# Attention prologue as one stream by blocks, and the global query's row moved up

## The reference

```python
q = proj(Wq, bq) / np.float32(np.sqrt(dh)); k = proj(Wk, bk); v = proj(Wv, bv)
sb = jnp.einsum('bhnqd,bhnkd->bhnqk', qb, kb) + bias[:, None]      # band of three blocks of 128
sg = jnp.einsum('bhsd,bhgd->bhsg', q, kg)                          # the global key
probs = jax.nn.softmax(jnp.concatenate([sg, sb_flat], axis=-1), axis=-1)
out = einsum(probs band, vb) + einsum(probs global, vg)
sfull = jnp.einsum('bhgd,bhsd->bhgs', qg, k)                       # the global query's row over all keys
out = out.at[:, :, g].set(einsum(softmax(sfull), v))
return out @ Wo.T + bo
```

## Time and profile before

| | |
|---|---|
| runs | 1120.85, 1123.35, 1115.32 us; median 1120.85 |
| profiled execution | 1120.8 us; its span 1119.1 us |
| busy over the span | PE 885.0 us (79%), DVE 632.5 (57%), ACT 576.6 (52%), POOL 479.3 (43%) |
| mean granted TensorE clock | 0.888 of 2.4 GHz |
| first pass | first projection 30.3 us, first transposition 52.6, first transposed softmax unit (L1282) 80.6, output projection (L1322) 173.5 |
| first projections of the other passes | 232.6, 546.5, 750.5 us |

### The profile page before, as it was taken

The page is one execution under the profiler, slowest core; times in us unless marked ns, Lnnn a source line. Parts: engine busy times, 40 slices in busy tenths (PEclk is TensorE's granted clock), DMA queues, the critical chain, the costliest instruction groups (busy, mean ns, idle before and its releaser), DMA issues.

```text
span 1119.1 us, 24365 instructions
## 1 busy us (share of the span) xinstructions
PE 885.0 (79%) x8585; PEld 663.0 (59%) x8585; DVE 632.5 (57%) x2094; ACT 576.6 (52%) x1633; POOL 479.3 (43%) x676
## 2 busy tenths in 40 slices
PE   2789999977999896681688998968899998585376
PEld 0567766746776565551366766647677575374376
DVE  2688834457884525534478855328986353645343
ACT  1449983245798443121266985326599633312254
POOL 4008874310687634212205875520388554312233
PEclk9889999979999996685799999988999889577699
DMA  3200000020000004003210000002000000400221
GB/s 93 73 5 4 3 18 1 1 71 8 4 3 14 6 0 170 0 1 104 62 52 3 3 3 17 0 12 67 3 4 3 17 1 1 170 1 18 92 77 39
DMA packets 25974, 34.29 MB, mean 31 GB/s; under 512 B 7460, under 2 KB 19590, under 8 KB 25560
## 3 DMA queue, kind: packets, MB, share of 16 engines
q1 hardware_dynamic: 22234, 27.44, 7.9%
q0 software_dynamic: 2272, 4.74, 1.4%
q10 hardware_dynamic: 1338, 0.44, 0.2%
HBM read 26.64 MB, written 5.73 MB: 29 GB/s over the span
## 4 chain that ended last, share of the span: by engine, by line
PE 52%; DVE 19%; issue 14%; ACT 5%; DMA 4%; POOL 3%; SPq 2%; POOLq 1%; ACTq 1%; DVEq 0%
PE bank L1328 6%; PE bank L1180 5%; PE bank L1282 5%; PE bank L1338 4%; PE bank L1339 4%; PE bank L1238 4%; PE bank L1308 3%; DVE nmx L912 3%; PE bank L1285 2%; ACT p L709 2%; PE bank L1197 2%; PE bank L1241 2%; DMA xt<-xs 2%; PE bank L1213 2%; DVE nat L846 1%
## 5 line engine op out<-in xcount | busy, mean ns | idle before, releaser
L567 POOL TENSOR_TENSOR p<-p 128x384 f16<-128x384 f32 (+1 forms) x320 | 270.5, 859 | 101.1 <-ACT p L709 94.5
L912 DVE TENSOR_REDUCE nmx<-bank 128x1 f32<-128x384 f32 (+1 forms) x384 | 187.0, 511 | 39.3 <-PE bank L1241 34.9
L708 ACT ACTIVATE p<-bank 128x384 f32<-128x384 f32 (+1 forms) x384 | 174.3, 454 | 46.0 <-PE bank L1285 35.8
L709 ACT ACTIVATE p<-bank 128x384 f16<-128x384 f32 (+1 forms) x384 | 174.9, 455 | 0.0
L1282 PE MATMUL bank<-stack 103*128 103x128 bf16 x1056 | 145.8, 222 | 8.2 <-ACT p L709 4.6
L1285 PE MATMUL bank<-bandb,idb 128*128 128x128 bf16 x672 | 135.6, 222 | 0.0
L1238 PE MATMUL bank<-stack 100*128 100x384 bf16 (+1 forms) x384 | 120.9, 321 | 5.9 <-DVE nmx L912 4.5
L524 POOL TENSOR_TENSOR rstd<-ve,colc 128x1 f32<-128x1 f32 x96 | 54.2, 565 | 152.6 <-DVE ve L799 152.4
L1308 PE MATMUL bank<-vst,p 128*128 128x49 bf16 x2112 | 115.8, 185 | 0.1
L1282 PEld LDWEIGHTS bank<-stack 103*128 103x128 bf16 x1056 | 88.7, 99 | 31.4 <-issue 16.1
L1241 PE MATMUL bank<-bandb,idb 128*128 128x128 bf16 x672 | 102.3, 223 | 0.0
(11 more groups left out here) (252 smaller groups left out, 1890.4 us busy)
## 6 DMA issues: line engine op xcount, KB each, us to landing
mwbs<-in_mwb SPq DMA_DIRECT2D x2, 2064.0 KB, 8.7
mw2s<-in_mw SPq DMA_DIRECT2D x2, 2048.0 KB, 13.0
xt<-xs SPq DMA_DIRECT2D x23, 129.0 KB
w2s<-in_w SPq DMA_DIRECT2D x4, 576.0 KB
xs<-zrow SPq DMA_DIRECT2D x16, 129.0 KB
lnrow<-in_lnr SPq DMA_DIRECT2D x4, 480.0 KB
stack<-mtr SPq DMA_DIRECT2D x96, 3.0 KB
wqb<-in_wqkv SPq DMA_DIRECT2D x6, 218.2 KB
```

The costliest lines, as they stand in the source:

```text
L567: nc.gpsimd.tensor_tensor(p2[:, u % RING, 0:w], p32[:, u % RING, 0:w], p1[:, u % RING, 0:w], ALU.subtract).then_inc(p2_pool, 1)
L708: nc.scalar.activation(p32[:, s % RING, 0:w], ps[2 + s % 3][:, 0:w], ACT.Exp).then_inc(p32_ready, 1)
L709: nc.scalar.activation(p1[:, s % RING, 0:w], ps[2 + s % 3][:, 0:w], ACT.Exp).then_inc(p1_ready, 1)
L912: nc.vector.tensor_reduce(nmx[:, vn % 3, h:h + 1], nat_bank(v)[:, 0:w], AX.X, ALU.max, negate=True).then_inc(max_done, 1)
```

## The change

The stages ahead of unit 0 become one list by blocks. For j = 0 to 8 each engine does the part of block j's projection, then in four parts (`PARTS`) what belongs to the transposition of block j - 1, and from j = 3 on one of the 24 early steps behind each part (`early_step`). The `sg.meet()` behind the transpositions is gone; TensorE waits for single semaphores. v has one bank, `ps[2]`, the transpositions two, `ps[3]` and `ps[4]`, now eight heads of one block at a time; the early maxima two, `ps[6]` and `ps[7]`. Of the three groups of a block ScalarE evicts the first and third, VectorE the second. The rest after the first piece stays in PSUM, in place, and ScalarE reads the middle piece from there. The places of the pieces are reordered so that the repeated ones lie side by side; GpSimd makes the copies (`again`), in four instructions per block. `nat` holds two blocks and lies in the tile `hid` of the MLP. The global query's row keeps its start at step 72; its later steps move up (exponential to 85, norm 86, transposition and `f12` 88 and 89, product with v 90 to 93, mask product 95, column sums 97, copies 98). The two halves lie side by side in `f12`, so that one matmul does both, and the mask product takes two instructions over 24 rows, with `own` for `bm`. In the diff, cut to its core, 16 columns of indentation are left out.

```diff
-Q_ROWS = ((0, 16, 32), (48, 64), (80,))
-K_ROWS = ((0, 48, 80), (16, 64), (32,))
+HI, MID = 0, DH
+Q_HI, Q_MID, Q_LO = 2 * DH, 4 * DH, 5 * DH
+K_HI, K_MID, K_LO = 4 * DH, 2 * DH, 3 * DH
+HG = 8
+PARTS = 4
...
-            return ps[v % 4] if v < LEAD else ps[v % 2]
+            return ps[6 + v % 2] if v < LEAD else ps[v % 2]
+
+        def early_step(j, part):
+
+            return -LEAD + PARTS * (j - 3) + part if j >= 3 else None
...
-    sg.meet()
-    for s in range(-LEAD, U + 18):
+
+    def step(s):
...
+    for j in range(NB + 1):
+        if j < NB:
+            q, k = nat[:, j % 2, 0:H, :], nat[:, j % 2, H:2 * H, :]
+
+            def again(t, at, src):
+                return nc.gpsimd.tensor_copy(
+                    t[:, :, at:at + 2 * DH].rearrange("p h (i d) -> p h i d", d=DH),
+                    t[:, :, src:src + DH].unsqueeze(2).to_broadcast([P, H, 2, DH]))
+
+            pool.wait_ge(qk_hi, j + 1)
+            again(q, Q_HI, HI)
+            again(k, K_HI, HI)
+            pool.wait_ge(qk_mid, j + 1)
+            nc.gpsimd.tensor_copy(q[:, :, Q_MID:Q_MID + DH], q[:, :, MID:MID + DH])
+            nc.gpsimd.tensor_copy(k[:, :, K_MID:K_MID + DH], k[:, :, MID:MID + DH]).then_inc(qk_again, 1)
+        for part in range(PARTS):
+            if early_step(j, part) is not None:
+                step(early_step(j, part))
+    for s in range(0, U + 18):
+        step(s)
...
-    for n in range(NB):
-        act.wait_ge(qk_mm, n + 1)
-        nc.scalar.activation(nat[:, n, :, 0:DH],
-                             ps[n % 2][:, 0:2 * D].rearrange("p (h d) -> p h d", d=DH),
...
-    for k in range(0, 2 * H, 2):
-        act.wait_ge(tr_mm, k + 1)
-        nc.scalar.activation(stack[0:NPIECE, k, :], psb[4 + k % 4][0:NPIECE, :],
-                             ACT.Copy).then_inc(ev_act, 1)
-    sg.meet()
-
-    for s in range(-LEAD, U + 18):
-        if s == ROW + 14:
+
+    def step(s):
+        if s == ROW + 13:
...
-        if s == ROW + 19:
+        if s == ROW + 16:
             act.wait_ge(ft_mm, 1)
-            nc.scalar.activation(f1[:, :, :], ps[0][:, 0:NB * H].rearrange("p (n h) -> p n h", h=H),
+            nc.scalar.activation(f12[:, :, 0, :], ps[0][:, 0:NB * H].rearrange("p (n h) -> p n h", h=H),
...
-        if s == U + 7:
+        if s == U + 2:
...
+    def evacuate(b, g):
+        act.wait_ge(tr_mm, 3 * b + g + 1)
+        nc.scalar.activation(
+            stack[0:NPIECE, g * HG:(g + 1) * HG, blk(b)],
+            psb[3 + (3 * b + g) % 2][0:NPIECE, :].rearrange("p (h t) -> p h t", t=P),
+            ACT.Copy).then_inc(ev_act, 1)
+
+    for j in range(NB + 1):
+        if j < NB:
+            act.wait_ge(qk_mm, j + 1)
+            if j >= 2:
+                act.wait_ge(tr_mm, 3 * (j - 1))
+            nc.scalar.activation(nat[:, j % 2, :, HI:HI + DH],
+                                 ps[j % 2][:, 0:2 * D].rearrange("p (h d) -> p h d", d=DH),
+                                 ACT.Copy).then_inc(qk_hi, 1)
+            act.wait_ge(v_mm, j + 1)
+            nc.scalar.activation(vst[:, j, :, 0:DH], ps[2][:, 0:D].rearrange("p (h d) -> p h d", d=DH),
+                                 ACT.Copy).then_inc(v_hi, 1)
+        for part in range(PARTS):
+            if part == 1 and j < NB:
+                act.wait_ge(qk_rest, j + 1)
+                nc.scalar.activation(nat[:, j % 2, :, MID:MID + DH],
+                                     ps[j % 2][:, 0:2 * D].rearrange("p (h d) -> p h d", d=DH),
+                                     ACT.Copy).then_inc(qk_mid, 1)
+                act.wait_ge(v_rest, j + 1)
+                nc.scalar.activation(vst[:, j, :, DH:2 * DH],
+                                     ps[2][:, 0:D].rearrange("p (h d) -> p h d", d=DH),
+                                     ACT.Copy).then_inc(v_mid, 1)
+            if part in (1, 3) and j >= 1:
+                evacuate(j - 1, part - 1)
+            if early_step(j, part) is not None:
+                step(early_step(j, part))
+    for s in range(0, U + 18):
+        step(s)
...
+    def global_key():
+        dve.wait_ge(kb_out, 16 * H)
+        dve.wait_ge(rows_in, 32)
+        dve.wait_ge(ev_act, 2)
+        dve.wait_ge(ev_dve, 1)
...
+                                ALU.mult, ALU.add).then_inc(glob_ready, 1)
+
+    def global_value():
+        dve.wait_ge(v0_mm, 1)
+        for g in range(2):
+            ins = nc.vector.tensor_tensor(v0d[:, g, :], ps[6 + g][0:2 * H, 0:GW], own[:, g, :], ALU.mult)
+        ins.then_inc(v0_ready, 1)
+
...
-        if s == ROW + 16:
+        if s == ROW + 14:
             dve.wait_ge(f_exp, 2)
...
-        if s == ROW + 20:
+        if s == ROW + 17:
             dve.wait_ge(f1_ready, 1)
-            nc.vector.tensor_tensor(f2[:, :, :], ps[0][:, 0:NB * H].rearrange("p (n h) -> p n h", h=H),
-                                    f1[:, :, :], ALU.subtract).then_inc(f2_ready, 1)
-        if s == U + 4:
+            nc.vector.tensor_tensor(f12[:, :, 1, :], ps[0][:, 0:NB * H].rearrange("p (n h) -> p n h", h=H),
+                                    f12[:, :, 0, :], ALU.subtract).then_inc(f2_ready, 1)
+        if s == U - 1:
             dve.wait_ge(og_mm, 1)
+
+            def by_piece(t):
+                return t.rearrange("p (h w) -> p h w", w=VW)[:, :, 0:3 * DH].rearrange(
+                    "p h (i d) -> p i h d", d=DH)
+
             for g in range(2):
-                v_ = ps[1 - g][0:H, 0:HH * VW].rearrange("p (h w) -> p h w", w=VW)
-                for i in range(3):
-                    ins = nc.vector.tensor_tensor(
-                        heads(og[:, i, :])[:, half(g), :], v_[:, :, i * DH:(i + 1) * DH],
-                        heads(bm[0:H, :])[:, half(g), :], ALU.mult)
+                ins = nc.vector.tensor_tensor(
+                    og[:, :, g * HH * DH:(g + 1) * HH * DH].rearrange("p i (h d) -> p i h d", d=DH),
+                    by_piece(ps[1 - g][0:2 * H, 0:GW]), by_piece(own[:, g, :]), ALU.mult)
             ins.then_inc(og_ready, 1)
...
+    for j in range(NB + 1):
+        if j == 3:
+            global_key()
+        if j < NB:
+            q, k = nat[:, j % 2, 0:H, :], nat[:, j % 2, H:2 * H, :]
+            r, rv = heads(ps[j % 2][:, 0:2 * D]), heads(ps[2][:, 0:D])
+            dve.wait_ge(qk_hi, j + 1)
+            nc.vector.tensor_tensor(r, r, nat[:, j % 2, :, HI:HI + DH], ALU.subtract).then_inc(qk_rest, 1)
+            dve.wait_ge(v_hi, j + 1)
+            nc.vector.tensor_tensor(rv, rv, vst[:, j, :, 0:DH], ALU.subtract).then_inc(v_rest, 1)
+        if j == 2:
+            global_value()
+        for part in range(PARTS):
+            if part == 1 and j < NB:
+                dve.wait_ge(qk_mid, j + 1)
+                nc.vector.tensor_tensor(q[:, :, Q_LO:Q_LO + DH], r[:, 0:H, :], q[:, :, MID:MID + DH], ALU.subtract)
+                nc.vector.tensor_tensor(k[:, :, K_LO:K_LO + DH], r[:, H:2 * H, :], k[:, :, MID:MID + DH],
+                                        ALU.subtract).then_inc(qk_lo, 1)
+                dve.wait_ge(v_mid, j + 1)
+                nc.vector.tensor_tensor(vst[:, j, :, 2 * DH:3 * DH], rv, vst[:, j, :, DH:2 * DH],
+                                        ALU.subtract).then_inc(v_lo, 1)
+            if part == 2 and j >= 1:
+                dve.wait_ge(tr_mm, 3 * (j - 1) + 2)
+                nc.vector.tensor_copy(
+                    stack[0:NPIECE, HG:2 * HG, blk(j - 1)],
+                    psb[3 + (3 * (j - 1) + 1) % 2][0:NPIECE, :].rearrange("p (h t) -> p h t", t=P)).then_inc(ev_dve, 1)
+            if early_step(j, part) is not None:
+                step(early_step(j, part))
+    for s in range(0, U + 18):
+        step(s)
...
+    def project(j):
+        if j >= 2:
+            pe.wait_ge(qk_lo, j - 1)
+        mm(ps[j % 2][:, 0:2 * D], xa[:, blk(j)], wqa[:, 0:2 * D], start=True, stop=False)
...
+        if j >= 1:
+            pe.wait_ge(v_lo, j)
+        mm(ps[2][:, 0:D], xa[:, blk(j)], wqa[:, 2 * D:3 * D], start=True, stop=False)
+        mm(ps[2][:, 0:D], xb[0:DHI + 1, blk(j)], wqb[0:DHI + 1, 2 * D:3 * D], start=False,
            stop=True).then_inc(v_mm, 1)
...
+    def turn(b, g):
+        if g == 0:
+            pe.wait_ge(qk_lo, b + 1)
+            pe.wait_ge(qk_again, b + 1)
+            if b >= 1:
+                pe.wait_ge(ev_dve, b)
+        else:
+            if 2 * b + g - 1 > 0:
+                pe.wait_ge(ev_act, 2 * b + g - 1)
+        for h in range(HG):
+            ins = nc.tensor.transpose(psb[3 + (3 * b + g) % 2][0:NPIECE, blk(h)], nat[:, b % 2, g * HG + h, :],
+                                      idb[:, :])
         ins.then_inc(tr_mm, 1)
-    sg.meet()
...
-        if s == ROW + 18:
+        if s == ROW + 16:
...
-            if s != ROW + 22 + n // 2:
+            if s != ROW + 18 + n // 2:
                 continue
             if n == 0:
                 pe.wait_ge(f2_ready, 1)
             for g in range(2):
-                for ft in (f1, f2):
```

(45 more changed lines are left out.)

106 lines of the change are left out of this document (20 added, 86 removed).

## The result

| | before | after |
|---|---|---|
| median of 16 runs each | 1122.3 us | 1110.5 us |
| ratio | | 0.988, 95% interval 0.986 to 0.990 |
| profiled execution, its span | 1120.8, 1119.1 us | 1108.6, 1106.8 us |

The change makes the kernel 1.2% faster. The forecast was 1090 us, 31 us less than before; 12 came. The range held the time; the gain was less than half of the forecast.

What follows compares the result with a forecast made beforehand. Three engines took turns as the bound before the first softmax unit, then the global row's serial chain at the end. Stream 23.3 us plus tail 8 us made 31.3 off 1120.8: forecast 1090 us, range 1072 to 1118.

Steps and rivals of the forecast that it cites:

- The pace of the stream: Projections, transpositions and maxima as one stream: the order of work, not any engine's sum, sets 5.0 us per block.
- Rivals 1 and 3: Stream: 1, chain in block longer, period 5.8 us, 1113 us, chance 0.15; 3, TensorE-bound, period 4.5 us, 1074 us, 0.15.
- rival 4: Before the first softmax unit: the DMA of the maxima's rows, 3 us later, replaces the engines as bound; 1101 us.
- Its length: First projection to first softmax unit: 44.2 us for 50.3 in pass one, 23.3 us saved over four passes.
- The tail: Global query's row at the attention's end: 4.6 us for 6.65, 2.0 saved per pass (bounds 1.0 and 3.3), 8 in all.
- 0.9 us of them shows: Global row's product matmuls, 2.2 us in steps paced by ScalarE and GpSimd: only 0.9 us adds to the time.
- the forecast's terms: Tail waits: 0.6 us ScalarE for the transposition, 0.83 last combination, 1.1 TensorE for last units; 1.08 mask product goes.
- Rival 2, the clock: TensorE at half clock in the new stream: 1173 us if throughout, 1140 us if 60% of it; chance 0.10.

Runs made afterwards that it cites:

- mid_late: The changed kernel with the middle piece of block 0's maxima rows one step later, behind ScalarE's share of block 7: 1102.5 us, ratio 0.982.
- unmerged: The changed kernel with the global row's products as 32 matmuls of 12 rows again for 16 of 24, at their new place: 1120.0 us, ratio 0.999.

## Why the prediction was wrong

Between the two profiled executions 19.1 us of the forecast gain are missing: 9.0 in the stream, 6.5 in the tail and 6.7 behind it, less 3.1 won where nothing was forecast.

**The pace of the stream** was right. First-piece copies stand 4.99 us apart from block 3 to 5 (5.0 forecast) and 5.3 in the next two blocks, where the forecast had added work too; the third group is released by ScalarE's eviction, TensorE idles 0.68 us there, and undoing that order took 0.46 us off the period. GpSimd's copies (0.51 us for 384 columns, 0.35 for 192) were nowhere a wait, and evictions in eight runs cost ScalarE 1.02 us and VectorE 0.68, the price of the earlier trace rows. Rivals 1 and 3 are out: the period was neither 5.8 us, nor TensorE's 4.5 before the order was changed. So is rival 4: the first softmax unit starts 0.24 us behind the last eviction, with no DMA in the chain ahead of it.

**Its length** was mis-sized, 45.9 to 47.1 us for 44.2, 9 us in all, the largest part of what is missing. In pass one 0.8 had gathered by the start of block 7, 0.1 us a block. Block 7 took 6.8 us for 6.2: ScalarE's wait came where I had put it, 3.6 us behind the projection, but VectorE's maxima, behind its own late pieces, then kept TensorE waiting 0.41 us more. Block 8 took 4.2 for 3.8. Passes two and four add about 1 us each for a half clock near block 8. Moving one instruction by a step (`mid_late`) gave back 6 us of it.

**The tail** was the failed step: "They fall in steps that ScalarE and GpSimd pace ... so 0.9 us of them shows". TensorE is the pace there. The steps are paced by ScalarE and GpSimd in the earlier trace rows only while no products are in them; the row of a step without the added work does not show who paces it with it. `unmerged` measures what 16 more matmuls cost at the new place, 2.4 us a pass: nothing of them is hidden, so of the 2.2 us that were left 1.3 more show than forecast. At nearly the same clock the sum comes out: for the kernel before (second pass) TensorE is busy 28.1 us of 30.8, in the changed kernel (first pass) 25.8 of 30.2, so 2.3 us less work and 1.7 us more idle. The idle time is much what the forecast's terms give (0.6, 0.83 and 1.1 less the 1.08 of the mask product, 1.45 us). In the traces it is 0.75 us around the transposition, where TensorE waits 2.08 us for the norm and for ScalarE, before 1.33, and 1.04 us for the last combination on VectorE, which stood under the column sums before. With the merged row at its old place TensorE is busy 26.1 us of 28.6: the same work without that idle time. So moving the row was the wrong half of the edit. Summed over passes with their different clocks, the change gave 0.4 us a pass, and the row alone -0.5, where the forecast's lower bound was 1.0. The output projection begins 93.3 us behind the first softmax unit (91 forecast).

The forecast priced no half clock in the tail. It falls on about two of the four product steps, 1.7 us each for 1.07 at the full clock, so some 1.2 us a pass go to it by my estimate. But three of the four tails of the kernel before had it too, at 0.94, 0.94 and 0.89, and no run took it away; what it cost the change alone is not shown.

**The stage behind** was not in the sum at all, and lost 6.7 us. Of these about 2.6 are the half clock at the start of the output projection, 0.86 us in each of three passes (before, it fell there in pass four only); 2.4 are the unchanged stretch, run twice. What is left, about 1.7 us, I have not placed.

**Rival 2, the clock**, was priced for the stream alone, where it came out at 0.94, 0.92, 0.94 and 0.92 for 0.86, 0.90, 0.90 and 0.85 before, though TensorE is busy for the same share of the first stretch (39.05 of 46.0 us, 42.62 of 50.3). By the Trainium skill, TensorE: Matmul & The Clock Gate, section "A second HAM failure mode: psum-queue depth-cycling", TensorE's short waits between groups of matmuls would make the clock go up and down in the stream. The trace disagrees in the main: TensorE waits for an eviction in every block, 0.3 to 1.5 us in pass one, and behind the first 6 us the clock is the full one to the end in passes one and three, and falls once, near block 8, in two and four.

Still open: what decides whether the clock falls at a given place. The kernel before and the stream with the old row run the same code from the row's scores on, and the first keeps a clock of 1.0 through the first tail while the second has 0.93. In the profiled executions of these fourteen kernels the unchanged stretch took 26.9 to 32.0 us, at clocks of 0.87 down to 0.68. I can tell which clock it had, but not from an edit which one it will get.

## What to carry to other kernels

Before work is put into steps that another engine paces, add it up for the engine that gets it: a step of 0.53 us that gets 0.52 us of matmuls took 1.07. An instruction moved up in its engine's list is worth nothing if what it waits for does not come sooner too: here it held everything behind it for 1.92 us. And compare a change of 1% by stages: code that nobody touched differed by up to 10 us between kernels.

## What was not expected of the hardware

The granted clock of an unchanged stretch is a price of its own: 23.4 us of matmuls at 0.87 and 28.4 us at 0.73, twice in a run. And GpSimd copies 384 bf16 columns in 0.51 us, less than the 0.72 us of its subtraction of 256 fp32 ones, which I had taken as the nearest row.
